# Fused dense stage of a graph network: the layer norm's root ahead of the second squares, its inverse and shift at the end of the iteration

## What is computed

```python
h = jnp.maximum(_layernorm(x, axis=-1), 0.0)
x = x + _L1_gnn_ref(h, src, dst, ...)
...
def _layernorm(x, axis=-1, eps=1e-05):
    m = jnp.mean(x, axis=axis, keepdims=True)
    v = jnp.var(x, axis=axis, keepdims=True)
    return (x - m) / jnp.sqrt(v + eps)
...
        h = gatv2_conv(x, s, d, Wl1, Wr1, att1, b1)
        h = layer_norm(h, g1, be1)
        h = jax.nn.relu(h + x)
        h2 = gatv2_conv(h, s, d, Wl2, Wr2, att2, b2)
        h2 = layer_norm(h2, g2, be2)
        return h2 + h
```

## Time and profile before

| | us |
|---|---|
| median of 3 runs | 4635.77 |
| lowest and highest | 4630.58, 4641.23 |
| the profiled execution, its own time | 4636.25 |
| its span | 4634.5 |
| node_chain in it, about | 852 to 1541 |
| busy in the span: PE, DVE, ACT, POOL | 3307.0, 3210.8, 2604.3, 2915.7 |

### The profile page before, as it was taken

One profiled execution on the slowest core, in us unless ns is written; L12 is line 12 of the kernel. 1 busy time (PEld: TensorE's weight loads), 2 busy tenths in 40 slices (PEclk: granted clock), 3 DMA queues, 4 the chain that ended last, 5 costly groups with the idle time before them and its releaser, 6 DMA issues. The chain is left out here.

```text
span 4634.5 us, 66260 instructions
## 1 busy us (share of the span) xinstructions
PE 3307.0 (71%) x15560; PEld 1990.1 (43%) x15560; DVE 3210.8 (69%) x10235; ACT 2604.3 (56%) x7608; POOL 2915.7 (63%) x2865
## 2 busy tenths in 40 slices
PE   2544288688888699985987999678856559973332
PEld 2444133477777334333663343245522235553331
DVE  2322299688888578876876888679978868863332
ACT  2322299588888577763774777446667725530000
POOL 6777677488887677756877875135577400037776
PEclk7766599899999899997998999889978879975555
DMA  8433388567776466656984545299979957653331
GB/s 327 117 98 87 120 282 279 179 239 243 238 243 216 152 213 209 215 171 199 327 269 135 166 157 163 79 311 334 328 257 346 325 143 230 225 174 98 98 96 53
DMA packets 549485, 942.99 MB, mean 203 GB/s; under 512 B 86253, under 2 KB 170248, under 8 KB 547204
## 3 DMA queue, kind: packets, MB, share of 16 engines
q1 hardware_dynamic: 481252, 800.20, 51.4%
q0 software_dynamic: 65856, 113.13, 9.2%
q10 hardware_dynamic: 2016, 25.69, 1.3%
HBM read 563.37 MB, written 381.14 MB: 204 GB/s over the span
## 5 line engine op out<-in xcount | busy, mean ns | idle before, releaser
L1163 DVE TENSOR_TENSOR conv_logits_leaky<-conv_logits_z,conv_logits_sloped 128x512 f32<-128x512 f32 x784 | 516.8, 687 | 111.7 <-ACT conv_logits_sloped L1097 103.1
L1097 ACT ACTIVATE conv_logits_sloped<-conv_logits_z 128x512 f32<-128x512 f32 x784 | 459.4, 596 | 176.3 <-PE conv_logits_z L1059 121.2
L1438 PE MATMUL conv_aggregate_part<-conv_aggregate_weighed,conv_wlc 128*128 128x512 f32 x784 | 360.1, 603 | 38.9 <-DVE conv_aggregate_weighed L1520 38.9
L1059 PE MATMUL conv_logits_z<-conv_logits_hdT,conv_logits_wsum 128*128 128x512 f32 x784 | 367.2, 612 | 15.1 <-DVE conv_logits_leaky L1163 13.1
L1066 PE MATMUL conv_logits_z<-conv_diffT,conv_logits_wl 128*128 128x512 f32 x784 | 352.9, 593 | 0.0
L748 PE MATMUL node_chain_o<-node_chain_ident,node_chain_biasT 128*128 128x128 f32 x784 | 220.5, 281 | 118.8 <-ACT node_chain_hT L844 117.2
L749 PE MATMUL node_chain_o<-node_chain_wmean,node_chain_hT 128*128 128x128 f32 x1568 | 273.8, 277 | 0.0
L1520 DVE TENSOR_TENSOR conv_aggregate_weighed<-conv_aggregate_alpha,conv_diffT 128x512 f32<-128x512 f32 x392 | 256.0, 713 | 10.0 <-DMA conv_aggregate_alpha<-ALPHA 10.0
L1930 PE MATMUL mean_edges_turned<-mean_edges_ident,mean_edges_hs 128*128 128x128 f32 x196 | 54.5, 434 | 278.0 <-DMA mean_edges_hs<-H,idx 278.0
L113 POOL DMA_INDIRECT gat_logits_hs<-H,idx x196 | 212.6, 1085 | 59.9 <-issue 58.0
L1972 DVE SCALAR_TENSOR_TENSOR mean_edges_rows<-mean_edges_back,mean_edges_half,mean_edges_base 128x128 f32<-128x128 f32 x196 | 55.3, 344 | 275.8 <-DMA out<-mean_edges_rows,idx 266.7
(11 more groups left out here) (297 smaller groups left out, 10609.0 us busy)
## 6 DMA issues: line engine op xcount, KB each, us to landing
conv_aggregate_alpha<-ALPHA SPq DMA_DIRECT2D x392, 256.0 KB, 5.2
HX<-node_chain_hx SPq DMA_DIRECT2D x98, 512.0 KB, 3.2
AGG<-gine_edges_zero ACTq DMA_DIRECT2D x14, 1792.0 KB, 36.1
gine_mlp_x<-x SPq DMA_DIRECT2D x98, 256.0 KB
gine_mlp_agg<-AGG SPq DMA_DIRECT2D x98, 256.0 KB
YT<-gine_mlp_yT SPq DMA_DIRECT2D x98, 256.0 KB, 4.4
node_chain_x<-x SPq DMA_DIRECT2D x98, 256.0 KB, 3.2
node_chain_yT<-YT SPq DMA_DIRECT2D x98, 256.0 KB, 2.7
```

The costliest lines, as they stand in the source:

```text
L1059: pe.matmul(z[h][:, :], wsum[:, h * D:(h + 1) * D], hdT[j % 3][:, :], start=True, stop=True).then_inc(z_done[0], 1)
L1097: act.activation(sloped[(H * (2 * j + c) + h) % S][:, :], z[h][:, :], ACT.Copy, scale=SLOPE).then_inc(sloped_made[c], 1)
L1163: dve.tensor_tensor(leaky[H * c + h][:, :], z[h][:, :], sloped[(H * (2 * j + c) + h) % S][:, :], ALU.max).then_inc(leaky_made[c], 1)
L1438: last = pe.matmul(part[n % 2][:, :], g.wlc[:, h * D:(h + 1) * D], weighed[n % 2][:, h, :], start=(h == 0), stop=(h == H - 1))
```

## The change

Two steps change place, each in one engine's list. On VectorE, inverse and shift (`norm.scales`) go from first in the list with lag 2 to the place between `scale(1)` and `sum_first` with lag 1: the same tile, late in the iteration before. On ScalarE, the norm's root goes from last in the list to the place between `copy_turned(0)` and `square(1)`, with the same lag 1.

```diff
--- before.py
+++ after.py
@@ -827,7 +827,7 @@
                     dve.wait_ge(scaled_made[0], n + 1)
                     dve.tensor_tensor(flat(scaled[0][n % 3]), flat(scaled[0][n % 3]), flat(base[0][n % 4]), ALU.add).then_inc(sum_made, 1)
 
-                sweep(N, [(2, lambda n: norm.scales(dve, n % NR, n + 1)), (0, batch_norm), (5, scale(0)), (1, take_rows), (9, scale(1)), (5, sum_first)])
+                sweep(N, [(0, batch_norm), (5, scale(0)), (1, take_rows), (9, scale(1)), (1, lambda n: norm.scales(dve, n % NR, n + 1)), (5, sum_first)])
 
             @block.scalar
             def _(act):
@@ -862,8 +862,8 @@
                     past(act, base_made[1], n - 3)
                     act.activation(h2[n % 4][:, :, :], scaled[0][n % 3][:, :, :], ACT.Relu).then_inc(h2_made, 1)
 
-                sweep(N, [(2, normalize), (4, square(0)), (6, relu), (3, copy_turned(0)), (8, square(1)), (7, copy_turned(1)),
-                          (1, lambda n: norm.root(act, n % NR, n + 1, eps))])
+                sweep(N, [(2, normalize), (4, square(0)), (6, relu), (3, copy_turned(0)),
+                          (1, lambda n: norm.root(act, n % NR, n + 1, eps)), (8, square(1)), (7, copy_turned(1))])
 
 
 class Masks:
```

## The result

| | before | after |
|---|---|---|
| median of 7 runs each, us | 4635.77 | 4649.65 |
| lowest and highest | 4630.58, 4641.23 | 4646.66, 4658.07 |
| ratio of the times, 95% interval | | 1.0032 [1.0021, 1.0044] |
| the profiled execution, its time and span | 4636.25, 4634.5 | 4646.66, 4644.9 |
| a steady tile of 512 nodes | 6.59 | 6.81 |

The kernel became 0.3% slower: 14 us, where +18 was forecast.

What follows compares the result with a forecast made beforehand. No engine is full; VectorE and ScalarE wait for each other. VectorE's own 5.72 us plus a 1.07 us block give a 6.79 us tile against 6.59: +0.20 x 88 = +18 us, so 4654 us, widened range 4628 to 4664.

Steps and rivals of the forecast that it cites:

- Wait (a): VectorE, L828 to L168: 0.62 us per tile waiting for ScalarE's root, which the change would remove.
- Wait (b): VectorE, L173 to L796: 0.25 us per tile in which the shift waits for GpSimd's addition L697 to end.
- The new block: VectorE's L828 or L796 would wait for the rest of GpSimd's addition L697: 1.07 us per tile.
- the two places left open: L697 gets in behind the shift or behind L828, so the blocked VectorE instruction is L828 or L796.
- The rule of the whole 1.27 us: Exclusive port lock for the whole addition: block 1.27 us less 0.05, tile 6.94 us, time 4667 us; not used.
- The tile: Steady tile of 512 nodes in the fused dense stage: VectorE 5.72 + 1.07 = 6.79 us against 6.59.
- ScalarE's wait: It would move from the normalisation L178 to the root L157, waiting for the moments about 1 us per tile.
- Rival 1: VectorE keeps the port through shift, L828 and L796: no block, ScalarE bounds at 5.81 us, 4567 us; chance 0.17.
- Rival 2: An even trade: the new block is only 0.86 us, tile 6.58 us, time 4635 us; chance 0.16.
- Rival 3: The root comes too early, waits for the moments and holds back squares and copy: near 4600 us; chance 0.03.
- The first tiles and the last eight: Tiles outside the 88 steady ones, with no shift beside L697: claimed to stay as they are.

Runs made afterwards that it cites:

- e4: Only ScalarE's half of the change (root early), VectorE's list as in the kernel before: 4630.87 us, ratio 0.9994 to the kernel before.
- e2: Changed kernel, with GpSimd's addition L697 also waiting for VectorE's first sum L828: 4566.91 us, ratio 0.9854 to the kernel before.
- e12: Changed kernel, with GpSimd's addition L697 cut to 4 of 512 columns per partition, waits kept: 4924.78 us, ratio 0.9842 to the kernel before.
- e13: The same kernel as e2, run on another chip: 4940.21 us, ratio 0.9877 to the kernel before.
- e10: Changed kernel, with GpSimd's addition L697 also waiting for the shift: 5010.14 us, ratio 1.0007 to the kernel before.
- e7: Changed kernel, with VectorE's first sum L828 moved ahead of the second scaling: 4659.41 us, ratio 1.0057 to the kernel before.
- e3: Kernel before, with GpSimd's addition L697 waiting for the next iteration's batch norm L796: 4988.56 us, ratio 0.9966 to the kernel before.
- e11: Kernel before, with GpSimd's addition L697 also waiting for VectorE's first sum L828: 5038.11 us, ratio 1.0072 to the kernel before.
- e8: Changed kernel, with VectorE's first sum L828 moved directly behind the first scaling: 5091.4 us, ratio 1.0165 to the kernel before.

## Why the prediction was right

- **Wait (a), 0.62 us, is gone.** So it was: no idle before L168 in the steady tiles. e4 shows that the early root alone does it.
- **Wait (b), 0.25 us, is gone as well**, because L173 gets past before L697: L173 at 0.11 us after the end of L820, L697 at 0.13.
- **The new block, forecast 1.07 us, is 1.08.** Of the two places left open it fell on L828, 0.06 us behind L697 (0.05 was the estimate). The rule of the whole 1.27 us, the Trainium skill's (SBUF — State Buffer, "SBUF: two separate sides"), is right on the exclusion and long by some 0.13: L828 ends at 1108.18, its own 0.68 us began by that at 1107.50, and L697 had started at 1106.36. So the record of an addition holds VectorE up for 1.14 us from its start.
- **The tile, forecast 6.79, is 6.81**, and 88 x 0.22 is 19 us.
- **ScalarE's wait moves to L157**: forecast about 1 us, measured 0.92.
- **Rival 1** (VectorE keeps the port, 4567 us) is not what happens. That e2 reaches its time by force, with 4566.91, is in part luck: the price was 88 x 0.78 = 69 us from ScalarE's 5.81, while e2's tile is 5.90, which gives 61, and the other 6 lie outside the steady tiles. With no block to speak of, in e12, the gain is 80. **Rival 2** (an even trade) is what the early root alone gives, in e4. Rival 3 did not occur.

One term was wrong: "The first tiles and the last eight have no shift with L697 beside it and stay as they are." They got shorter. In the first tiles, where TensorE and ScalarE still fill the chain, VectorE's L168 sat waiting for a root far down ScalarE's list. The same tile in the trace of before, and then in that of the changed kernel:

```profile
891.97 0.18 DVE L168 RECIPROCAL node_chain_norm_rstd<-node_chain_norm_std 128x4 f32<-128x4 f32 x1 [2.69 <-ACT node_chain_norm_std L157]
```

```profile
889.56 0.18 DVE L168 RECIPROCAL node_chain_norm_rstd<-node_chain_norm_std 128x4 f32<-128x4 f32 x1 [0.81 <-ACT node_chain_norm_std L157]
```

The first L828 starts 1.7 us sooner, at 894.4 for 896.1. (That much need not be the change's: from the stage's first L796 it takes 41.1 us for 43.0 here, but in e2 and e13, which are one program, 41.6 and 43.1.) The next five tiles take 27.8 us for 29.4, the last five 21.8 for 23.2. That is 4.7 us, and the few longer tiles in between lost about 1 us of their length. So the last L828 of the stage is late by 13.2 us (1537.5 for 1524.3) and not by 19, which is the 14 us of the result within its interval. The forecast of +18 was right in its main term (a block of 1.07 for 1.08, +19 us over the steady tiles) and missed this one of some 5 us, of which 3 are clear of the doubt above.

## What to carry to other kernels

An idle gap on an engine is not yet a gain: ask what runs beside it and would collide with what moves in. Of two engines that share a port, list all instructions of both that need it, in the order in which they ask. The place to win is where the engine off the critical path can be made to wait, and here one semaphore wait on GpSimd turned a loss of 14 us into a gain of 67. The same wait beside the old order of VectorE's list lost 33, so move and wait have to be tried together.

A blocked instruction shows as busy. When an engine's busy share rises though its work did not, look for a line whose duration has grown by about the length of another engine's instruction.

## What the runs showed of the hardware that I had not expected

- VectorE does not keep the port from one instruction to the next: in e10 L698 asked while L829 ran, and got it ahead of L797, which came 0.36 us later.
- Close starts are not settled by the lead in the records. GpSimd was first with a recorded lead of 0.06 us over L828 here (1106.36, 1106.42) and over L796 in e7, in every steady tile, while at 900.52 it also led by 0.06 and VectorE went first. The latter is no single case: it holds for the first three tiles of that kind in each of before, e3, e4, e7 and e11, 15 in all, with leads of 0.03 to 0.06 us. In those 15 no shift stood directly ahead of L828, and the addition was L692 and not L697. Which of the two decides was not tried.
- The block is 1.08 us on L828 (after), and 0.96 to 0.97 on L796 with L697 in the same place, 0.06 us ahead (e7, e8). Why the single input is held up 0.1 us less is open.
- Of the three chips of the experiments one differs from the other two by 8% in the whole kernel (4634 and 5005 us) and not at all in the steady tile (5.90 us in e2 and e13); the same edit was worth 67 us on the one (e2) and 65 on the other (e13).
